# Releasing the PSUM buffer of local-attention scores after the row minima, in the planner of a fused transformer kernel

## What is computed

```python
qkv = h @ wqkv
q, k, v = jnp.split(qkv, 3, axis=-1)
q = l2norm(q) * qs
k = l2norm(k) * ksc
q, k = rotary_xpos(q, k)
...
sim = jnp.einsum('bhwid,bhwjd->bhwij', bq, bk)      # windows of 128, own window and the one before
mask = (i < j) | (i > j + WINDOW) | (j == -1)
sim = jnp.where(mask, -jnp.finfo(sim.dtype).max, sim)
attn = jax.nn.softmax(sim, axis=-1)
out = jnp.einsum('bhwij,bhwjd->bhwid', attn, bv)
x = x + o @ wo
...
h = h @ w1 + b1
a, g = jnp.split(h, 2, axis=-1)
h = a * jax.nn.gelu(g, approximate=False)
x = x + h @ w2 + b2
```

## Time and profile before

| | |
|---|---|
| median of 3 runs | 4717.62 us (4715.44 to 4721.88) |
| the profiled execution | 4717.21 us, its span 4715.3 us |
| PE busy | 4207.5 us, 89% of the span |
| DVE busy | 3324.7 us, 71% |
| ACT busy | 2555.6 us, 54% |
| POOL busy | 1603.4 us, 34% |
| chain that ended last | PE 67%, DVE 19%, ACT 6%, issue 5%, POOL 2% |

### The profile page before, as it was taken

One profiled execution on the slowest core, in us unless ns is written; L12 is line 12 of the kernel. 1 busy time (PEld: TensorE's weight loads), 2 busy tenths in 40 slices (PEclk: granted clock), 3 DMA queues, 4 the chain that ended last, 5 costly groups with the idle time before them and its releaser, 6 DMA issues.

```text
span 4715.3 us, 65711 instructions
## 1 busy us (share of the span) xinstructions
PE 4207.5 (89%) x23120; PEld 2616.4 (55%) x23120; DVE 3324.7 (71%) x7849; ACT 2555.6 (54%) x5482; POOL 1603.4 (34%) x1816
## 2 busy tenths in 40 slices
PE   7888888999999999988888878888999999999997
PEld 4545455655655655655555455554565665665654
DVE  5555566676676676648899999988677666667662
ACT  4444444444444444437888888876444444444441
POOL 2122235454454554430000010012554454454441
PEclk9999999999999999997888898888999999999998
DMA  2000000000001000000000000100000000000000
GB/s 72 10 5 15 18 5 12 3 5 3 21 10 28 7 10 12 18 17 19 21 21 21 17 26 21 32 19 18 19 3 5 3 22 10 28 16 19 12 19 20
DMA packets 63094, 78.31 MB, mean 17 GB/s; under 512 B 15344, under 2 KB 47520, under 8 KB 62768
## 3 DMA queue, kind: packets, MB, share of 16 engines
q1 hardware_dynamic: 62768, 74.12, 5.5%
HBM read 36.37 MB, written 12.58 MB: 10 GB/s over the span
## 4 chain that ended last, share of the span: by engine, by line
PE 67%; DVE 19%; ACT 6%; issue 5%; POOL 2%; DMA 0%; SPq 0%; POOLq 0%; DVEq 0%; ACTq 0%
PE wide L782 48%; PE o_ps L782 8%; PE turn_ps L785 6%; PE wide L785 4%; DVE x L1213 3%; DVE w_up L1326 2%; DVE prob L1338 2%; DVE x L1332 2%; PE turn_ps L782 1%; DVE w_up L1311 1%; POOL prob L1542 1%; DVE hid L1332 1%; DVE resid L1398 1%; DVE x L1430 1%; DVE k_t L1273 1%
## 5 line engine op out<-in xcount | busy, mean ns | idle before, releaser
L782 PE MATMUL wide<-x,w_up 128*128 128x512 f32 (+5 forms) x2560 | 864.4, 549 | 27.8 <-DVE x L1430 20.6
L782 PE MATMUL wide<-w_in,x_t 128*128 128x512 f32 (+2 forms) x1920 | 818.0, 570 | 57.1 <-ACT turned L1076 43.8
L1542 POOL TENSOR_SCALAR prob<-prob,st 128x256 f32<-128x256 f32 (+1 forms) x1024 | 449.3, 459 | 989.2 <-DVE st L1362 988.7
L1145 ACT ACTIVATE prob<-prob,st 128x256 f32<-128x256 f32 (+1 forms) x1024 | 479.4, 472 | 315.6 <-DVE st L1349 315.6
L782 PEld LDWEIGHTS wide<-w_in,x_t 128*128 128x128 f32 x1920 | 344.1, 193 | 411.1 <-issue 403.5
L782 PEld LDWEIGHTS wide<-x,w_up 128*128 128x128 f32 (+2 forms) x2560 | 370.9, 195 | 297.9 <-issue 253.1
L782 PE MATMUL o_ps<-pt,v 128*32 128x128 f32 (+2 forms) x5120 | 508.8, 345 | 26.6 <-DVE pt L1375 10.2
L785 PE MATMUL turn_ps<-ident,prob 128*128 128x128 f32 x2480 | 407.4, 283 | 93.5 <-issue 40.3
L1515 POOL TENSOR_TENSOR sines<-raw,rot 128x512 f32<-128x512 f32 x256 | 352.4, 1397 | 334.8 <-ACT raw L1073 334.8
L785 PEld LDWEIGHTS turn_ps<-ident,prob 128*128 128x128 f32 x2480 | 285.2, 142 | 319.5 <-issue 247.5
L1523 POOL TENSOR_TENSOR rn<-ss,minus_half 128x16 f32<-128x16 f32 x128 | 410.0, 3203 | 151.8 <-DVE ss L1259 145.0
(11 more groups left out here) (139 smaller groups left out, 7362.1 us busy)
## 6 DMA issues: line engine op xcount, KB each, us to landing
kept<-resid SPq DMA_DIRECT2D x16, 512.0 KB, 2.6
x<-kept SPq DMA_DIRECT2D x16, 512.0 KB, 3.3
w_up<-hid SPq DMA_DIRECT2D x64, 128.0 KB, 2.2
x<-hid SPq DMA_DIRECT2D x64, 128.0 KB, 2.4
shifted<-resid SPq DMA_DIRECT2D x32, 224.0 KB
w_in<-in_f_wqkv SPq DMA_DIRECT2D x4, 1536.0 KB, 6.9
w_up<-in_f_w SPq DMA_DIRECT2D x4, 1492.0 KB, 7.5
resid<-in_x SPq DMA_DIRECT2D x8, 512.0 KB, 8.6
```

What stands on the lines that cost most here:

```text
L782: return eng.matmul(out, lhsT, rhs, start=start, stop=stop, skip_group_check=True)
L1145: last = eng.activation(pr[:, local_span(t)], pr[:, local_span(t)], ACT.Exp, bias=sm[:, t:t + 1], scale=-1.0, accum_out=sm[:, 4 + t:5 + t])
L1542: last = eng.tensor_scalar(pr[:, local_span(t)], pr[:, local_span(t)], sm[:, 8 + t:9 + t], 1.0, ALU.mult, ALU.mult)
```

## The change

One condition is added in `buffer_at`: when the holder of a buffer is a `score` part of stage "f", `exp` is left out of the readers whose end frees the buffer, so that the planner counts the buffer free after `low`. Stage "a" is untouched, and so are the costs, the due times, the instructions and the semaphore waits.

```diff
@@ -451,7 +451,8 @@
             at = 0.0
             if holder is not None:
                 hk, hu, hi = holder
-                last = [(r, hu, 0 if hk in ("proj", "down") else hi) for r in READERS[hk]]
+                last = [(r, hu, 0 if hk in ("proj", "down") else hi) for r in READERS[hk]
+                        if (hk, r, stage_of(hu)) != ("score", "exp", "f")]
                 if hk == "turn_a" and stage_of(hu) == "b":
                     last.append(("pt_b", hu, hi))
                 last = [r for r in last if r in parts]
```

## The result

The changed kernel takes **4638.78 us** (median of 4 runs, 4629.82 to 4642.2) against 4717.35 (4715.44 to 4721.88) for the kernel before: a ratio of 0.9829, 95% interval 0.9812 to 0.9846, so 1.7% less time. The forecast was 4646.0 with a range of 4630 to 4676. The profiled execution took 4629.82 us and was the fastest of the four.

What follows compares the result with a forecast made beforehand. PE was taken to bound the 26 repeating units, with about 4.5 us idle each. Gains of 50.2, 15.6 and 10 less 4 lost take 71.8 us off the 4715.3 us span, giving 4646 us; range 4630 to 4676.

Steps and rivals of the forecast that it cites:

- Part 1: `qk` 1 on PE no longer waits for the square of `raw` 0: 1.93 us a unit, 50.2 us gained.
- Part 2: POOL's `sin` of tile 2 leaves DVE's `nrm_f` earlier, so `xt2` waits less: 0.6 us a unit, 15.6 us gained.
- Part 3: MLP ending a double stage: `up_h` 1 no longer waits for `hid` 0; 5 us each in units 23 and 47.
- Part 4: What becomes late, mainly DVE's `join` 1, by 0.15 us a unit: 4 us lost; later `gelu` costs nothing.
- Rival 1: `join` 1 late by `nrm_f`'s gain, only the `raw` wait goes: 4671; shares chance 0.24 with two other rivals.
- only part 1 holds: Sign in the changed profile: `res2` distance in repeating units 86.1 us, instead of the forecast 85.6.
- Rival 2: Shared port: DVE's `join` 1 waits for POOL's `wt`, 0.87 us a unit, 4669; shares 0.24 with two others.
- The clock: Half-clock falls in 8 of 26 units, about 1.0 us each: fewer expected, counted as nothing, 8 us either way.
- Units 8 and 32: Beginnings of the "f" stages, also re-ordered: nothing counted, 3 us either way each.
- The sum: Profiled span of 4715.3 us loses 71.8, making 4643.5; forecast time 4646 us, 1.5% less.
- Rivals 3, 4 and 5: PE's wait reappears elsewhere (4671 or no change; within 0.24 shared); late `gelu`, slower (0.03); change does nothing (0.04 no change).

Runs made afterwards that it cites:

- part 1 alone: Kernel before, only `qk` 1 moved to head 1's score buffer and head 3's scores to `qk` 0's, in the 26 repeating units: 4676.99 us, ratio 0.9907.
- without part 2: Changed kernel with POOL's `rstd_f` back in front of `wt` 3 in the 26 repeating units: 4666.15 us, ratio 0.9882.
- the edit of `up_h`: Kernel before with `up_h` 1 and `up_h` 2 of units 22 and 46 exchanging buffers: 4720.11 us, one run.

## Point by point: why the prediction was right

**Part 1, right to the hundredth.** 1.93 us a unit predicted, 1.92 measured for `qk` 1, in the changed kernel and in the two experiments that do or undo it alone. `qk` 1 started 0.44 us behind `turn_a`, as said.

**Part 2, right.** 0.6 predicted, 0.56 by the medians and 0.55 by undoing it. `sin` 2 starts before `nrm_f`'s third instruction and `xt2`'s wait is 1.27 us (said: about 1.2).

**Part 3, right in size, not complete.** The buffer of `up_h` 1 gives 6.0 and 4.6 us, against 5 each, by one execution and with the clock's share in it. Units 22, 23, 46 and 47 together lost 18.1 us; 3 of them are the clock in unit 23. The remaining 4 to 5 us are the other reorderings there, which I had not costed.

**Part 4, the term that was mis-sized.** 0.15 us a unit for a late `join` 1, measured 0.63 in 24 of the 26 units: some 15 us lost instead of 4. The mechanism stood there, with `inv` 1 behind `low` 2 and `ss` 1 earlier, and `res` does start at once behind `join`. What the step left out is what lies beside what: moving `ss` 1 ahead of `join` 0 puts `join` 0 beside `wt` 1, and `wt` 1 is on this path. It became 1.03 us longer, `sin` 1 another 0.43, and on DVE `cos` 1 beside `sin` 1 2.1 us. The step names none of these longer durations. The rest of part 4 held: nothing from the later `gelu`, 0.1 from `turn_b` 2.

**Rival 1 came true in the repeating unit, though not in the time.** It said that `join` 1 on DVE is late by as much as `nrm_f` gains. The unit gained 0.56 us at `xt2` and lost 0.63 at `qk` 2, and the distance of the `res2` is 86.07 us: the 86.1 that the prediction gave for "only part 1 holds", not its own 85.6. Part 2 did work, as the run without it shows, but its gain was eaten by part 4. The rival's 4671 us did not come, because of gains elsewhere (below).

**Rival 2, the port: it did not happen to the pair that it named, but to its neighbours.** The rival had `join` 1 lose 0.87 us beside `wt` 2. Both instructions of `join` 1 together took 0.07 us more than before (1.19 and 1.33, where it was 1.22 and 1.23), and `wt` 2 was stretched to 2.69. `join` 0 beside `wt` 1 is the same case: its multiplication 1.38, `wt` 1 2.77 (2.97 in the earlier trace rows). I used this only to show that DVE is safe and did not ask whether POOL's loss is on the path, nor what happens to the other pairs. Beside a `sines` row DVE does lose: `cos` 1 took 3.43 us instead of 1.31. The Trainium skill ("SBUF — State Buffer", "Who interferes with whom") says that the one which issues second blocks fully until the other is done. The runs agree on `nrm_f`: its instructions take 0.33 us alone and 1.30 to 1.41 beside a `sines` row, and the experiment that takes the row away gets all of it back.

**The clock, counted as nothing, was worth up to 9.7 us** in the 26 units, just over the bound of 8. All eight falls are gone. The prediction's 1.0 us for one fall was right.

**Units 8 and 32, also counted as nothing:** 69.2 to 64.9 and 77.2 to 72.6 us, 8.9 together, where the bound was 3 each. PE is busy for 57.5 us in unit 8 of the changed kernel, for 58.1 before, so nearly all of it is less waiting. The gain is the same in every run: 69.1 to 69.3 us in the four kernels with the orders of before, 64.8 to 64.9 in the five with the changed ones. Which of the moved parts brings it, no experiment takes apart.

**The sum.** Predicted: 71.8 us off the span. Measured: 87.4, made of 58.8 (26 units), 8.9 (units 8 and 32), 18.1 (22, 23, 46, 47), 4.5 ("b"), and some 3 us back in units 1 to 7 and at the end. Of the excess of 15.6, some 9 belong to this execution alone, since the median of the changed kernel is 9 us above it. The medians differ by 78.6, 7 more than forecast. So the total came out close because two errors nearly cancel: 12.7 us too much gain from the repeating unit (part 4), and in this execution some 27 us of gain in the clock (9.7), units 8 and 32 (8.9) and the rest of the last units (8.1 over the 10 put down), that I had left at zero. That these nearly cancel is luck: the forecast for the repeating unit, 85.6 us, was too low by 0.5. Rivals 3, 4 and 5 are out: part 1 holds in full, no wait of over 1 us came up in the repeating unit, and `gelu`'s delay brought no wait.

## What to carry to other kernels

When the instructions are the same and only their order or buffers change, PE's waits at fixed places can be priced to a few hundredths of a microsecond from two timeline rows, one with and one without the wait. Check then which POOL and DVE instructions come to lie beside each other: the pair's loss may fall on the engine that seems unimportant, and it counts if that engine feeds the next join. Here it turned the whole gain of part 2 into nothing. And ask of each wait what stretches the instruction that is waited for: moving one independent instruction of the other engine out of the way gave as much here as the better buffer for `qk` 1 did.

## What the runs showed of the hardware

**Where the clock falls.** The granted clock fell from 2.4 to 1.2 GHz for 3.4 us in 8 of the 26 repeating units before, in 5 with part 1 alone, in 3 without part 2 (once for 6.8 us), in 7 with the edit of `up_h`, and in none of the five others (the changed kernel among them), all in one execution of each. The kernels with falls are the ones in which PE waits about 1.8 us or more for `nrm_f` in every repeating unit, in front of the short transpositions of `xt2`. In three of the others that wait is 1.1 to 1.3 us in most units, with 1.5 to 2.2 us in four to six units and still no fall; in the other two it is nearly gone. Two of the others keep the 1.7 us wait in front of `qk` 1, between matmuls of 512 columns, and do not fall there. So in this kernel the falls go with the one wait and not with PE's idle time as a whole. A fall makes its unit about 1 us longer. Why these falls come in some units only, with the same order in each, stays open.

**What the pairs cost.** DVE's multiplication of two SBUF operands beside POOL's four `wt` instructions: POOL 1.74 to 2.77 us (2.97 in one place), DVE 1.23 to 1.38 at most. DVE's two `cos` instructions beside POOL's two `sines`: DVE 1.31 to 3.43 us, POOL 2.50 to 3.91. DVE's `nrm_f` instructions beside POOL's `sines`: 0.33 to 1.41 us.
